# Latent attention on fp32 strips of 32 partitions, row sums by products of ones on TensorE

## Chip, cores and metric

One core of one Trainium2 chip runs the whole program. The metric is device time in microseconds, the median of a few executions. Times inside the program are counted from the start of the profiled execution's span.

## The reference

A tensor x of 2048 tokens by 128 features, fp32, goes through eight residual layers: an RWKV layer, a mixture of experts, causal attention with rotation (16 heads of 8), the mixture again, one full-attention head, a second mixture, latent attention, and that mixture again. Each is `x = x + layer(layernorm(x))`. The change concerns the seventh. Cut to what matters:

```python
q = (x @ wq).reshape(B, T, 2, 4, 128)          # 2 groups of 4 query heads
k_lat = (x @ wk_down).reshape(B, T, 2, 32)     # one latent key and value of 32 per group
v_lat = (x @ wv_down).reshape(B, T, 2, 32)
k, v = k_lat @ wk_up, v_lat @ wv_up
scores = where(causal, q @ k.T / sqrt(128), lowest)
y = softmax(scores) @ v
return y.reshape(B, T, 1024) @ wo
```

The kernel folds wk_up into wq and wv_up into wo when it starts, so that a head's query, key and value have 32 elements here.

## The kernel before

Queries are cut into NC = 4 chunks c of 512, keys into tiles kj of 128. A **unit** is one key tile against one query chunk for the four heads of a group g; causality leaves (c+1)*4 units per chunk and group, 80 in all. Of each chunk's units four lie on the diagonal and cover 512, 384, 256 and 128 queries. Scores are made with keys on partitions, exponentiated to the tile PT by ScalarE (L1418, two heads at a time), and weighted by the values on TensorE (L1374, four heads in four column strips of 32, into PSUM bank 4).

The softmax needs each query's maximum beforehand. So TensorE also makes the scores with queries on partitions, 128 queries by up to 512 keys an item (L1304, with a mask added by L1308 on the diagonal), and VectorE reduces each (L1538). These **maxima** pass through a ring of three PSUM banks (5, 6, 7): TensorE waits on `ring_free` for a bank, VectorE on `ring_full` for its data. The negated maxima are turned by TensorE and enter the scores as three more rows of the product. `make_plan` writes out one order for all engines: for each unit scores of heads 0 and 1, some ring items, scores of heads 2 and 3, some ring items, the weighting of the unit before, the rest of the ring items. Engines work in that order and wait for each other on semaphores.

The class `CausalHeads` serves this layer and the rotated one. Queries and keys are split into three bf16 parts each; the parts of four source chunks go out to a DRAM tensor (L1629) and come back stacked as 96 rows (L1598), so that one bf16 product of 96 rows holds three part products. Scores take two products a head (99 rows, the last three being the maxima, and 96 rows, L1355), a maximum takes one:

```python
for j in (2 * p, 2 * p + 1):
    for m in range(self.NP):
        r = self.rows + (3 if m == 0 else 0)
        ins = pe.matmul(k.PS[:, j, q0:CH], self.K[0:r, g % 2, j % self.kheads, m, kj * P:(kj + 1) * P],
                        self.Q[0:r, g % 2, j, m, c * CH + q0:(c + 1) * CH],
```

Row sums: GpSimd adds three heads of PT into the tile acc, VectorE the fourth (L1460, L1462), and after a chunk's last unit TensorE sums acc over partitions (L1324), VectorE takes the reciprocal of 128x512 (L1568) and multiplies (L1570), TensorE makes the output product (L1333), VectorE adds it to X (L1579). VectorE also splits the negated maxima (L1551 to L1554). Groups are the outer loop, chunks the inner. The layer norm that follows needs all four chunks.

## Time and profile before

| | us |
|---|---|
| median of 3 runs | 1944.66 |
| lowest and highest | 1942.96, 1948.3 |
| span of the profiled execution | 1933.1 |
| median less span: what lies around the span | 11.6 |
| latent stage, first projection to the next layer norm's start | 1362.5 to 1846.9 |

The profiled execution's own time is known by its span alone, from the first to the last instruction. Rows read "start, length, engine, line, operation, out<-in, shapes, count", and in brackets how long the engine had been idle and on what. PE is TensorE, DVE VectorE, ACT ScalarE, POOL GpSimd, SP the queue that issues DMAs. An fp32 product shows as two MATMUL instructions, a bf16 one as one. A row with a count is several instructions merged, from the first start to the last end.

### The profile page before, as it was taken

What the parts mean: (1) busy time and instruction counts of PE and PEld (TensorE: products, weight loads), DVE (VectorE), ACT (ScalarE), POOL (GpSimd) and SP (SyncE); (2) the same over time, 40 slices, a digit from 0 to 9 for tenths busy, and PEclk for the clock granted to TensorE, in tenths of its full rate; (3) what the DMA queues carried; (4) which work ended last, traced back from release to release, by engine and by line L of the source; (5) the groups of instructions that cost most, each with busy time, mean ns of one, the idle gap of its engine ahead of it and who ended that gap; (6) DMA issues with size and microseconds to landing.
All of it is one profiled execution on the core that took longest, in us unless ns stands there. A gap on an engine that the chain in (4) does not pass through costs nothing.

```text
span 1933.1 us, 25832 instructions
## 1 busy us (share of the span) xinstructions
PE 1601.7 (83%) x8863; PEld 807.4 (42%) x8863; DVE 1180.5 (61%) x2315; ACT 786.5 (41%) x1031; POOL 818.4 (42%) x987
## 2 busy tenths in 40 slices
PE   4766699758999899999799789989545898988779
PEld 2222466412333333332466567766212333333256
DVE  5887633578788787883333333342355878897951
ACT  2222233343565565667333344444212343334433
POOL 2224646464554635455463644000001577456900
PEclk8788699867999999999799999979656898889979
DMA  4000000151000303000000000000143000000000
GB/s 139 1 0 0 1 1 0 59 121 29 2 2 12 41 3 51 2 2 1 1 1 0 0 1 0 0 1 0 49 117 96 1 1 1 1 1 1 1 1 22
DMA packets 31585, 36.86 MB, mean 19 GB/s; under 512 B 8606, under 2 KB 24703, under 8 KB 31362
## 3 DMA queue, kind: packets, MB, share of 16 engines
q1 hardware_dynamic: 27906, 29.29, 6.4%
q10 hardware_dynamic: 3520, 6.29, 1.6%
q8 instruction: 61, 1.00, 0.2%
q14 instruction: 34, 0.28, 0.1%
q0 software_dynamic: 64, 0.00, 0.0%
HBM read 26.10 MB, written 8.91 MB: 18 GB/s over the span
## 4 chain that ended last, share of the span: by engine, by line
PE 61%; DVE 16%; DMA 7%; SPq 3%; issue 2%; ACT 2%; ACTq 0%; DVEq 0%
PE PS L943 9%; PE PS L1355 9%; PE PS L931 9%; PE PS L1304 8%; PE PS L1374 8%; DVE sb_latent_acc L1462 3%; DMA sb_rope_K<-rope_parts 3%; PE PS L1723 3%; PE PS L1741 3%; SPq L1629 2%; DVE sb_latent_mp L1538 2%; DMA latent_parts<-sb_latent_parts 2%; DVE sb_rope_mp L1538 2%; DVE sb_latent_rec L1568 1%; PE PS L1735 1%
## 5 line engine op out<-in xcount | busy, mean ns | idle before, releaser
L1538 DVE TENSOR_REDUCE sb_rope_mp<-PS 128x1 f32<-128x512 f32 (+3 forms) x560 | 345.0, 669 | 76.5 <-PE PS L1308 36.9
L1418 ACT ACTIVATE sb_rope_PT<-PS 128x1024 f32<-128x1024 f32 (+3 forms) x320 | 273.3, 895 | 223.0 <-PE PS L1359 121.7
L1462 POOL TENSOR_TENSOR sb_latent_acc<-sb_latent_acc,sb_latent_PT 128x1536 f32<-128x1536 f32 (+3 forms) x72 | 223.2, 3101 | 72.4 <-ACT sb_latent_PT L1418 68.8
L1418 ACT ACTIVATE sb_latent_PT<-PS 128x1024 f32<-128x1024 f32 (+3 forms) x160 | 140.2, 895 | 243.3 <-PE PS L1359 80.9
L995 DVE SCALAR_TENSOR_TENSOR sb_X<-PS,sb_gates,sb_X 128x128 f32 (+1 forms) x320 | 90.1, 344 | 241.3 <-PE PS L943 241.2
L1304 PE MATMUL PS<-sb_rope_K,sb_rope_Q 96*128 96x512 bf16 (+3 forms) x640 | 211.7, 371 | 30.2 <-ACT sb_rope_V L1399 18.3
L1538 DVE TENSOR_REDUCE sb_latent_mp<-PS 128x1 f32<-128x512 f32 (+3 forms) x280 | 174.3, 666 | 46.2 <-PE PS L1304 32.5
L576 POOL TENSOR_SCALAR sb_pbelow<-sb_pa,sb_ptrial 128x512 f32<-128x512 f32 x124 | 197.0, 1599 | 6.4
L583 POOL TENSOR_TENSOR sb_pbelow<-sb_pbelow 128x1024 f32<-128x1024 f32 (+1 forms) x248 | 181.7, 733 | 19.6
L931 PE MATMUL PS<-sb_HT,sb_w 128*128 (+1 forms) x384 | 182.3, 612 | 3.6 <-DVE sb_seed L514 1.9
L1355 PE MATMUL PS<-sb_rope_Q,sb_rope_K 99*128 99x512 bf16 (+3 forms) x640 | 179.4, 352 | 1.4 <-ACT sb_rope_PT L1418 0.9
L1355 PE MATMUL PS<-sb_latent_Q,sb_latent_K 99*128 99x512 bf16 (+7 forms) x640 | 160.3, 372 | 8.3 <-ACT sb_latent_PT L1418 8.3
L1304 PE MATMUL PS<-sb_latent_K,sb_latent_Q 96*128 96x512 bf16 (+3 forms) x320 | 111.4, 393 | 63.4 <-ACT sb_latent_V L1399 23.3
L1460 POOL COPY sb_latent_acc<-sb_latent_PT 128x1536 f32<-128x1536 f32 x8 | 13.2, 1655 | 335.7 <-ACT sb_latent_PT L1418 287.0
L972 ACT ACTIVATE sb_moe_hidden<-PS,sb_vec 128x512 f32<-128x512 f32 x128 | 87.8, 687 | 159.4 <-PE PS L931 155.2
L1374 PE MATMUL PS<-sb_rope_PT,sb_rope_V 128*9 128x512 f32 (+3 forms) x1280 | 148.6, 536 | 0.1
L1304 PEld LDWEIGHTS PS<-sb_rope_K,sb_rope_Q 96*128 96x128 bf16 x640 | 59.5, 99 | 181.9 <-issue 94.2
L943 PE MATMUL PS<-sb_w0b,sb_moe_hidden 128*128 128x128 f32 x1024 | 131.3, 281 | 0.0
L943 PEld LDWEIGHTS PS<-sb_w0b,sb_moe_hidden 128*128 128x128 f32 x1024 | 119.1, 191 | 14.5 <-issue 14.5
L1462 DVE TENSOR_TENSOR sb_latent_acc<-sb_latent_acc,sb_latent_PT 128x512 f32<-128x512 f32 (+3 forms) x72 | 105.3, 1463 | 10.2 <-ACT sb_latent_PT L1418 9.7
L589 POOL TENSOR_TENSOR sb_ptot<-sb_ptot,sb_prank 128x8 f32<-128x8 f32 x31 | 6.1, 198 | 226.4 <-issue 226.4
L831 POOL TENSOR_TENSOR sb_rw_kvj<-sb_rw_k,sb_rw_vj 128x512 f32<-128x512 f32 x32 | 44.3, 1389 | 133.8 <-ACT sb_rw_vj L814 96.7
(291 smaller groups left out, 2438.7 us busy)
## 6 DMA issues: line engine op xcount, KB each, us to landing
latent_parts<-sb_latent_parts SPq DMA_DIRECT2D x36, 128.0 KB
sb_rope_Q<-rope_parts SPq DMA_DIRECT2D x9, 384.0 KB
rope_parts<-sb_rope_parts SPq DMA_DIRECT2D x24, 128.0 KB, 2.4
sb_rope_tab<-in_rotation SPq DMA_DIRECT2D x1, 2048.0 KB, 8.6
sb_rope_K<-rope_parts SPq DMA_DIRECT2D x6, 256.0 KB
sb_latent_Q<-latent_parts ACTq DMA_DIRECT2D x2, 768.0 KB
sb_latent_Q<-latent_parts SPq DMA_DIRECT2D x1, 1536.0 KB, 19.1
sb_rope_Q<-rope_parts ACTq DMA_DIRECT2D x6, 192.0 KB
```

Source lines behind the costliest of these rows:

```text
L576: ch.mark(g.tensor_scalar(self.below[:, w, s, :], self.a[:, w, :], tr[:, 2 * w + s:2 * w + s + 1], None, ALU.is_lt))
L583: ch(g.tensor_tensor(bl[:, :, 0:n], bl[:, :, 0:n], bl[:, :, n:2 * n], ALU.add))
L931: pe.matmul(k.bank(b), self.w1(e, m), x, start=True, stop=True).then_inc(self.hid[b], 1)
L943: ins = pe.matmul(k.PS[:, 4 + b, i * P:(i + 1) * P], self.g[:, b, m, i * P:(i + 1) * P], self.w2(e, m), start=False, stop=(m == M - 1), sk ...
L972: s.activation(self.g[:, e % 2, m, :], k.bank(b), self.func, bias=self.b1(e, m)) \
L995: ins = v.scalar_tensor_tensor(xi, k.PS[:, 4 + b:5 + b, i * P:(i + 1) * P], gate, xi, ALU.mult, ALU.add)
L1304: ins = pe.matmul(k.PS[:, bank, at:at + w], self.Q[0:self.rows, g % 2, j, 0, q0:q0 + P], self.K[0:self.rows, g % 2, j % self.kheads, 0, kc ...
L1355: ins = pe.matmul(k.PS[:, j, q0:CH], self.K[0:r, g % 2, j % self.kheads, m, kj * P:(kj + 1) * P], self.Q[0:r, g % 2, j, m, c * CH + q0:(c ...
L1374: ins = pe.matmul(k.PS[32 * j:32 * j + self.vcols, 4, q0:CH], v, self.PT[:, u % 2, j, q0:CH], start=(kj == 0), stop=(kj == last))
L1418: s.activation(self.PT[:, u % 2, 2 * p:2 * p + 2, q0:CH], k.PS[:, 2 * p:2 * p + 2, q0:CH], ACT.Exp, scale=self.scale).then_inc(self.exps[p ...
L1462: eng.tensor_tensor(acc, acc, new, ALU.add).then_inc(self.added[who], 1)
L1538: v.tensor_reduce(self.mp[:, n % 2, kc, heads[0]:heads[-1] + 1, i], k.PS[:, bank, 0:len(heads) * w].rearrange("p (h k) -> p h k", h=len(he ...
```

## The change

`StripHeads` takes the place of `CausalHeads` for this layer. Q and K stay fp32 in SBUF and never go to DRAM: each head's 32 elements lie on partitions 32j to 32j+31, and the latent key is written four times below itself (by a weight `wkrep` that repeats its columns). A score or maximum is one fp32 product of 32 rows, a **row strip** of the array. Maxima are one head each (320 items, before 280, some of which held several heads), in head order 2, 3, 0, 1. The negated maxima, split on GpSimd, are added by a bf16 product of 3 rows a head. Masks are written first and the product added to them. Row sums are made for every unit: a ring item `part` multiplies PT by ones in four column strips, VectorE adds it to S; after a chunk two DMAs and a reciprocal of 128x16 give the factors, which `den` spreads over partitions. The order of chunks and groups is swapped (chunks outer), maxima per unit go from 4.5 to 5, PT has 3 buffers instead of 2.

```diff
+    def make_plan(self):
+...
+            if u < total:
+                plan.append((u, "scores0"))
+            plan += ring(mine[:a])
+            if u < total:
+                plan.append((u, "scores1"))
+            plan += ring(mine[a:b])
+            if 1 <= u <= total:
+                plan.append((None, ("part", u - 1)))
+                plan.append((u - 1, "weighted"))
+            plan += [(u, it) for it in relays[u]]
+            plan += ring(mine[b:])
+...
+    def pe_scores(self, pe, u, p):
+...
+        if diag:
+            for j in pair:
+                pe.matmul(k.PS[:, j, q0:q0 + P], k.identb[:, :], k.mask_kq[:, :], start=True, stop=False,
+                          skip_group_check=True)
+        for j in pair:
+            strip = slice(32 * j, 32 * j + 32)
+            pe.matmul(k.PS[:, j, q0:CH], self.K[strip, g, kj * P:(kj + 1) * P],
+                      self.Q[strip, g, c * CH + q0:(c + 1) * CH], start=not diag, stop=False, skip_group_check=True)
+        for j in pair:
+            rows = slice(32 * j, 32 * j + 3)
+            pe.matmul(k.PS[:, j, q0:CH], k.onesb[rows, :], self.negT[rows, n % 2, q0:CH], start=False, stop=True,
+                      skip_group_check=True).then_inc(self.scores[p], 1)
+...
+    def pe_item(self, pe, item, bank):
+        k, kind = self.k, item[0]
+        if kind == "max":
+            _, n, i, kc, j = item
+            c, g = self.seq[n]
+            strip = slice(32 * j, 32 * j + 32)
+            w = CH if kc < c else (i + 1) * P
+            q0 = c * CH + i * P
+            if kc == c:
+                pe.matmul(k.PS[:, bank, w - P:w], k.identb[:, :], k.mask_qk[:, :], start=True, stop=False,
+                          skip_group_check=True)
+            return pe.matmul(k.PS[:, bank, 0:w], self.Q[strip, g, q0:q0 + P], self.K[strip, g, kc * CH:kc * CH + w],
+                             start=kc < c, stop=True, skip_group_check=True)
+...
+        if kind == "part":
+...
+            for j in range(4):
+                ins = pe.matmul(k.PS[32 * j:32 * j + 32, bank, q0:CH], k.ones_col, self.PT[:, u % self.PTS, j, q0:CH],
+                                start=True, stop=True)
+            return ins
+...
+        if kind == "part":
+            n, c, g, kj, q0 = self.unit(item[1])
+            if kj == 0:
+...
+                v.tensor_copy(self.S[:, n % self.NS, :], k.bank(bank)).then_inc(free, 1)
+            else:
+                self.emptied(v, ("part", item[1] - 1))
+                v.tensor_tensor(self.S[:, n % self.NS, q0:CH], self.S[:, n % self.NS, q0:CH], k.PS[:, bank, q0:CH], ALU.add) \
+                    .then_inc(free, 1)
+...
-            a = CausalHeads(k, "latent", ln, 2, sources + [(k.wkv[:, :, :].rearrange("p a l -> p (a l)"), None)], (qb, kb), 96, 1,
-                            k.wkv[:, 1, :], 2, 32, float(P ** -0.5), k.wy, d["latent_parts"], False, True, 4.5)
+            a = StripHeads(k, "latent", ln, 5.0)
```

On TensorE, in the middle of the stage before, a full unit stands like this: a maximum (K and Q read), four products for the scores of two heads, a maximum, the other four, a maximum, and the weighting of the unit before by the values V.

```order
L1304 MATMUL PS<-sb_latent_K,sb_latent_Q 128x512
L1355 MATMUL PS<-sb_latent_Q,sb_latent_K 128x512 x4
L1304 MATMUL PS<-sb_latent_K,sb_latent_Q 128x512
L1355 MATMUL PS<-sb_latent_Q,sb_latent_K 128x512 x4
L1304 MATMUL PS<-sb_latent_K,sb_latent_Q 128x512
L1374 MATMUL PS<-sb_latent_PT,sb_latent_V 32x512 x4
```

The same place after: two maxima (L1893), the scores of two heads (L1863, strips 0 and 1) with the rows of their negated maxima (L1867), two maxima, scores of strips 2 and 3, a maximum, then the row sums by ones (L1908, cst holds them) ahead of the weighting (L1878).

```order
L1893 MATMUL PS<-sb_latent_K,sb_latent_Q 128x512 x2
L1863 MATMUL PS<-sb_latent_Q,sb_latent_K 128x512 x2
L1867 MATMUL PS<-sb_latent_negT,sb_onesb 128x512 x2
L1893 MATMUL PS<-sb_latent_K,sb_latent_Q 128x512 x2
L1863 MATMUL PS<-sb_latent_Q,sb_latent_K 128x512 x2
L1867 MATMUL PS<-sb_latent_negT,sb_onesb 128x512 x2
L1893 MATMUL PS<-sb_latent_K,sb_latent_Q 128x512
L1908 MATMUL PS<-sb_latent_PT,sb_cst 32x512 x4
L1878 MATMUL PS<-sb_latent_PT,sb_latent_V 32x512 x4
```

Eight bf16 products for scores became four fp32 and four short-rowed bf16 ones, and four column-strip products were added. At a diagonal block a mask of the full array (L1891) now stands ahead of every maximum:

```order
L1891 MATMUL PS<-sb_mask_qk,sb_identb 128x128
L1893 MATMUL PS<-sb_latent_K,sb_latent_Q 128x384
L1891 MATMUL PS<-sb_mask_qk,sb_identb 128x128
L1893 MATMUL PS<-sb_latent_K,sb_latent_Q 128x384
L1863 MATMUL PS<-sb_latent_Q,sb_latent_K 128x512 x2
```

At the start of the stage TensorE had the four chunks' projections apart, each waiting for the splitting of the one before, and the values among them; now the projections stand in a row, then the values (L1826), and the first maxima:

```order
L1819 MATMUL PS<-sb_HT,sb_wc 128x512 x2
L1822 MATMUL PS<-sb_HT,sb_wkrep 128x512 x2
L1826 MATMUL PS<-sb_wkv,sb_HT 128x64 x16
L1891 MATMUL PS<-sb_mask_qk,sb_identb 128x128
L1893 MATMUL PS<-sb_latent_K,sb_latent_Q 128x128
```

Of the plan after, counted: 39 maxima stand ahead of the first unit (32 of them diagonal ones of chunk 0), and 281 among the units, five to a unit, 96 of them diagonal. 23 of the 80 units have no maximum, the last 19 among them.

## Rows read from the trace of the kernel before

**Rows 1.** The page: span, busy time, TensorE and its granted clock in 40 slices.

```profile
span 1933.1 us, 25832 instructions
...
PE 1601.7 (83%) x8863; PEld 807.4 (42%) x8863; DVE 1180.5 (61%) x2315; ACT 786.5 (41%) x1031; POOL 818.4 (42%) x987
...
PE   4766699758999899999799789989545898988779
...
PEclk8788699867999999999799999979656898889979
```

**Rows 2.** Windows of the latent stage: busy time and instructions, granted clock, DMA share.

```profile
core 0: us, PE busy (x) PEld busy (x) DVE busy (x) ACT busy (x) POOL busy (x), PEclk, DMA share, GB/s
1362.50:1427.50 65.00, 23.35 (x56) 9.57 (x56) 15.79 (x25) 16.53 (x32) 0.00 (x0) 0.58 0.29 85
1427.50:1475.80 48.30, 26.88 (x99) 9.14 (x100) 28.99 (x59) 1.31 (x2) 0.00 (x0) 0.57 0.59 148
1475.80:1555.50 79.70, 69.56 (x419) 29.29 (x418) 69.09 (x99) 28.49 (x34) 39.75 (x16) 0.89 0.00 1
1555.50:1775.70 220.20, 191.35 (x1173) 77.14 (x1172) 182.23 (x262) 85.94 (x101) 144.50 (x49) 0.91 0.01 1
1775.70:1835.30 59.60, 46.59 (x284) 14.51 (x281) 54.13 (x22) 29.00 (x33) 50.33 (x16) 0.96 0.00 1
```

**Rows 3.** Timeline of the stage's start: start, length, instructions, idle before and releaser.

```profile
1362.51 3.78 PE L1265 MATMUL PS<-sb_HT,sb_wc 128*128 128x512 f32 x4 [0.69 <-ACT sb_HT L245]
...
1367.10 3.68 PE L1273 MATMUL PS<-sb_wkv,sb_HT 128*128 128x64 f32 x32
...
1369.31 65.97 SPq L1629 DMA_DIRECT2D latent_parts<-sb_latent_parts  x36
...
1427.58 0.29 PE L1304 MATMUL PS<-sb_latent_K,sb_latent_Q 96*128 96x128 bf16 x1 [23.29 <-ACT sb_latent_V L1399]
```

**Rows 4.** The tile of exponentials: nanoseconds least/median/most, first and last start.

```profile
L1418 ACT ACTIVATE sb_latent_PT<-PS x160: 377/1024/1042, 1475.8 to 1834.9; 128x1024 f32<-128x1024 f32 x112, 128x768 f32<-128x768 f32 x16, 128x512 f32<-128x512 f32 x16, 128x256 f32<-128x256 f32 x16
L1462 POOL TENSOR_TENSOR sb_latent_acc<-sb_latent_acc,sb_latent_PT x72: 992/3460/3819, 1482.5 to 1836.2; 128x1536 f32<-128x1536 f32 x48, 128x1152 f32<-128x1152 f32 x8, 128x768 f32<-128x768 f32 x8, 128x384 f32<-128x384 f32 x8
```

**Rows 5.** Timeline of TensorE in one full unit among maxima.

```profile
1552.93 1.06 PE L1374 MATMUL PS<-sb_latent_PT,sb_latent_V 128*32 128x512 f32 x8
...
1554.37 1.04 PE L1355 MATMUL PS<-sb_latent_Q,sb_latent_K 99*128 99x512 bf16 x4
1555.24 0.38 PE L1304 MATMUL PS<-sb_latent_K,sb_latent_Q 96*128 96x512 bf16 x1
1555.46 1.03 PE L1355 MATMUL PS<-sb_latent_Q,sb_latent_K 99*128 99x512 bf16 x4
1556.33 0.38 PE L1304 MATMUL PS<-sb_latent_K,sb_latent_Q 96*128 96x512 bf16 x1
1556.64 1.06 PE L1374 MATMUL PS<-sb_latent_PT,sb_latent_V 128*32 128x512 f32 x8
```

**Rows 6.** Timeline of a unit without maxima.

```profile
1804.78 1.94 ACT L1418 ACTIVATE sb_latent_PT<-PS 128x1024 f32<-128x1024 f32 x2 [1.91 <-DVE sb_latent_acc L1462]
...
1805.86 1.96 PE L1355 MATMUL PS<-sb_latent_Q,sb_latent_K 99*128 99x512 bf16 x8 [0.89 <-ACT sb_latent_PT L1418]
...
1808.64 1.94 ACT L1418 ACTIVATE sb_latent_PT<-PS 128x1024 f32<-128x1024 f32 x2 [1.92 <-DVE sb_latent_acc L1462]
```

**Rows 7.** VectorE, groups by line and shape: busy us, mean ns, idle before.

```profile
L1538 DVE TENSOR_REDUCE sb_latent_mp<-PS 128x1 f32<-128x512 f32 x224 | 143.7, 681 | 36.1 <-PE PS L1304 32.5 <-PE PS L1308 2.9
...
L1568 DVE RECIPROCAL sb_latent_rec<-PS 128x512 f32<-128x512 f32 x8 | 26.8, 3351 | 5.8 <-PE PS L1324 5.8
...
L1498 DVE TENSOR_TENSOR sb_latent_x<-PS,sb_latent_parts 128x512 f32<-128x512 f32 x12 | 8.3, 692 | 49.1 <-ACT sb_latent_parts L1392 49.1
```

**Rows 8.** Timeline of the stage's end.

```profile
1835.46 0.66 PE L1374 MATMUL PS<-sb_latent_PT,sb_latent_V 128*32 128x128 f32 x8 [1.48 <-ACT sb_latent_PT L1418]
...
1846.89 0.87 DVE L197 BATCH_NORM_STATS2 sb_stats<-sb_X 128x6 f32<-128x128 f32 x4 [0.31 <-DVEq L1582]
```

More of the change, by code:

```diff
@@ L98, in __init__ @@
         self.den_rope = self.cst[:, 3 * P:4 * P]
+        self.den_strip = self.cst[:, 15 * P:16 * P]
         self.ones_col = self.cst[:, 4 * P:4 * P + 32]
@@ L116, in bank @@
         return self.PS[:, b, 0:cols]
-N_CST = 5 + 8 + 2
+N_CST = 5 + 8 + 2 + 1
 class NormMemory:
@@ L290, in __init__ @@
         k.wc = sb("wc", [P, 8, 32])
+        k.wkrep = sb("wkrep", [P, 2, 4, 32])
         k.wy = sb("wy", [P, 2, P])
@@ L442, in gpsimd @@
         g.tensor_copy(k.mask_kq[:, :], k.cst[:, (6 + 8) * P:(7 + 8) * P]).then_inc(self.ready, 1)
+        for i in range(2):
+            g.tensor_copy(k.wkrep[:, i, :, :], k.wkv[:, 0, 32 * i:32 * i + 32].rearrange("p (a l) -> p a l", a=1)
+                          .broadcast_to([P, 4, 32])).then_inc(self.ready, 1)
     def tensor(self, pe):
@@ L447, in tensor @@
         pe.wait_ge(s.ready, 1)
-        pe.wait_ge(self.ready, 4)
+        pe.wait_ge(self.ready, 6)
         n = 0
@@ L1881, in constants @@
     c[:, 14 * P:15 * P] = np.where(r[:, None] > r[None, :], MASKED, 0.0)
+    c[:, 15 * P:16 * P] = (r[:, None] // 32 == r[None, :] // 32) & (r[:, None] % 32 == 0)
     c[:, CST_ORDER:] = 8 - np.arange(8)
@@ L1987, in latent_attention @@
             ln = norm()
-            qb = [(0, 0, 0, 2), (0, 64, 0, 1), (1, 0, 0, 3)]
-            kb = [(0, 0, 0, 1), (0, 32, 0, 2), (1, 0, 2, 1), (1, 32, 1, 1), (1, 64, 0, 1)]
-            sources = [(k.wc[:, 4 * g:4 * g + 4, :].rearrange("p h l -> p (h l)"), None) for g in range(2)]
-            a = CausalHeads(k, "latent", ln, 2, sources + [(k.wkv[:, :, :].rearrange("p a l -> p (a l)"), None)], (qb, kb), 96, 1,
-                            k.wkv[:, 1, :], 2, 32, float(P ** -0.5), k.wy, d["latent_parts"], False, True, 4.5)
+            a = StripHeads(k, "latent", ln, 5.0)
             with ExitStack() as arena:
@@ L2042, in scratch @@
     d["rope_parts"] = nc.dram_tensor("rope_parts", (2, 16, 3 * 8, T), BF16).ap()
-    d["latent_parts"] = nc.dram_tensor("latent_parts", (3, 4, 3 * 32, T), BF16).ap()
 def kernel(**inputs):
```

324 lines of the change are left out of this document (added).

## Prediction

> **What bounds the kernel now.** I read the page first: TensorE is busy 83% of the span and VectorE 61% [rows 1]; no other stage changes, so I looked at the latent stage in windows. It has two parts. From the first projection to the first exponential, 1362.5 to 1475.8, lie 113.3 us in which TensorE is busy 36% and 56% of the time at a granted clock of 0.57 to 0.58, and the DMA share is 0.29 and 0.59 [rows 2]. The timeline says why: the issue queue is busy with stores of the parts for 65.97 us, and the first maximum comes at 1427.58, after 23.29 us of idle [rows 3]. That is the trip through DRAM. From the first exponential, 1475.8, to the end of the last, 1835.3, lie 359.5 us for 80 units [rows 2, 4], 4.5 us a unit.
>
> In this loop the reader is to see three periods. A full unit among maxima takes 3.71 us (1552.93 to 1556.64, weighting to weighting), and TensorE stands nearly end to end in it [rows 5]: it is the bound there. A unit without maxima takes 3.86 us (1804.78 to 1808.64), while TensorE needs some 3: the chain of waits goes through the additions, and the exponential waits 1.92 us on them [rows 6]; GpSimd's take 3.46 us in the median [rows 4]. At chunk ends VectorE's reciprocals (3351 ns each) and splits stop the ring [rows 7].
>
> **Prices.** A bf16 product of 512 columns starts 0.22 us after the one before: four take 1.04, of which the last one's own record is 0.38 [rows 5]. So a record runs 0.165 beyond its streaming. Four fp32 products in column strips are eight instructions in 1.06 us [rows 5]; less 0.165 that is 0.87, two passes of 0.43 each, all four strips at once. I take 0.85 of streaming for a row strip of 32 rows too, which no row shows; alone it is four times the bf16 product of 96 rows, 0.22, that it replaces, and only four strips at once make it equal. From the end of a full-array product's streaming (1556.33 + 0.22) to the start in column strips (1556.64) lie 0.09 us [rows 5]; I take 0.09 for each change of tiling. VectorE's reduction is 0.68 in itself [rows 7], about 0.61 in a row.
>
> **Removed and gained: the start.** Two cold projections take 3.78 as now [rows 3], fourteen more at 0.86 are 12.0, the values 3.7 [rows 3], their copy 1.2: 20.7. Then 32 diagonal maxima of chunk 0: a product of 128 to 512 columns (0.21 to 0.85, mean 0.53), a mask of 0.05, two changes of tiling 0.18, and all in a row since a mask uses the whole array: 0.77 each, 25. Seven more are 4, split, turn and copy of the maxima 4, the first scores 1.3. Sum 55 to 57, against 113.3: **-57**. Nothing hides this: the first exponential waits for all of it. At the program's start 64 KB more of constants are loaded and GpSimd makes two copies more, long before their use; I put both at nothing (the whole setup waits for the constants, but they are one of many loads).
>
> **Added: the loop.** Row sums and weighting: eight column-strip products, 1.75, and two changes of tiling, 0.19: 1.94 a full unit. The rest is nine fp32 products (four scores, five maxima) and four short bf16 ones over four strips. In the order written out, the strips of maxima are 2, 3, 0, 1 round and round, five a unit, so four phases occur. If an instruction may start only when those before it have started: with the first maxima on 2 and 3 they run beside the scores of strips 0 and 1 to 0.85, the rows of maxima to 1.07; the next two need strips 0 and 1, and the second of them also the first bank of the ring, which comes free at 1.8 (data at 1.09, reduction 0.68); scores of strips 2 and 3 beside it to 2.87; the fifth to 3.7. The other three phases collide more (4.7, 4.35, 4.3), mean 4.3, a period of **6.2**. If a busy strip doesn't hold up the others, the ring still does, and I get 3.75 and **5.7**. I take 5.95. The rows show strips at once only for columns; this is the main choice.
>
> Diagonal maxima come in fours: four at 0.77, one full 0.85, two pairs of scores at 1.07, less 0.6 where a maximum's product runs beside scores, and 1.94: **7.4**.
>
> - 185 full maxima are 37 units' worth, x 5.95: 220
> - 96 diagonal ones are 19.2 units' worth, x 7.4: 142
> - masks of the 32 diagonal units, four of 0.05 and four changes each: +18
> - 14 of those units cover fewer queries, 1.6 each: -22
> - without maxima: 13 full units at 3.2 (all four scores at once 1.07, 1.94, and a wait for the second exponential), 10 short ones at 2.5: 67
> - factors, output products and turns, 3.5 for each of 8 chunks: +28. The two DMAs are five to seven units away from their use and hidden; with that cover gone they would cost about 4 a chunk.
>
> Sum 453, against 359.5: **+93.5**. VectorE has 5 x 0.61 and an addition of about 0.69 (its subtraction from PSUM has that length [rows 7]), 3.75 in a unit of 5.95: no bound any more. ScalarE has 2.0. GpSimd's additions cost nothing in the dense units that TensorE bounds, and their removal is worth 0.65 in each of 13 units; it is in the sum.
>
> **The end.** Now 11.4 us from the last weighting (1835.46) to the next statistics (1846.89), with the long reciprocal [rows 8]. After, the reciprocal is of 128x16 but two DMAs are exposed; I put it at 1 less.
>
> Together 93.5 - 57 - 1 = +35.5. Against the profiled span 1933.1 that is 1968.6; the median shown lies 11.6 above the span, so **1980 us**.
>
> **A rule weighed.** The Trainium skill (TensorEngine Tiling (Array Packing), Tiling Modes) says that changing the tiling mode drains the engine. It speaks against this change, which adds masks of the full array among row strips; the column rows agree (0.09), for row strips no row shows it. The skill (TensorE: Matmul & The Clock Gate, Part 3) gives 3.07x for four row strips, not 4x; by that the overlapped part, 37 x 3.75, would be 1.3 times as long, an estimate of 2022 in all.
>
> **Rivals.**
> - *Faster.* Changes between row strips and the full array cost nothing (128 diagonal maxima x 0.18 and 32 x 0.36: -35) and strips run at once as far as the ring lets them (5.25 a full unit: -26): 1919. The changes alone give 1945, so it decides only with both, or with either and shorter diagonal units. For it: masks are short, and weights may load behind running products. Against: the 0.09 in rows 5.
> - *No change.* A loop of 415 to 420 instead of 453 just pays back the start: 1945.
> - *Maxima don't overlap with anything*, since each waits for a bank and signals by itself: 5 x 0.85 + 2 x 1.07 + 1.94 = 8.3 a full unit, +89: 2069. For it: the rows show overlap only for products that stand in a row without waits.
> - *Row strips don't run at once at all:* 10.5 a full unit, 10.1 a diagonal one, 6.2 without maxima, together some +265: 2245. Against: column strips do.
>
> **How the numbers follow.** Chances: the forecast (slower by a few per cent) 0.45, faster 0.31, no change 0.07, maxima alone 0.11, no overlap 0.06. 0.3%, or 6 us, is about what a measurement of this kernel can tell. The range reaches from below the faster rival, 1905, to above the third, 2075. The forecast's own range is 1955 to 2020 (periods of 5.25 to 7 for a full unit). Faster 0.31, same 0.07, slower 0.62.
>
> **What would show it.** The first exponential at about 1419 instead of 1475.8, with no stores of parts. TensorE at over 0.9 in the loop, granted clock near 1. Full units with five maxima 5.7 to 6.2 apart, diagonal ones 7 or more, the last ones 3.2. A gap of about 0.09 on both sides of each mask. Two maxima of neighbouring strips starting less than 0.2 us apart. The prediction is wrong if dense full units are nearer to 5 than 6, or if masks stand in the stream without gaps.

## The result, and the profile after

| | us |
|---|---|
| before, median of 4 runs on the same chip | 1946.24 (1942.96 to 1948.3) |
| after, median of 4 runs | 2117.8 (2110.47 to 2120.16) |
| ratio, 95% interval | 1.087 (1.0836 to 1.0905) |
| span of the profiled execution after | 2108.4 |
| forecast | 1980 (1905 to 2075) |

The change costs 171 us where 35 were forecast. The direction was right, the size was not, and the range missed. In one experiment below (few row sums) three of the four executions took 32 to 50 us longer than the fourth at a lower granted clock, and the traced one is the longest of them; so no ratio is given for it, and times are compared with its fastest execution.

The page of the changed kernel, the lines that answer to [rows 1]:

```profile
span 2108.4 us, 27826 instructions
...
PE 1879.6 (89%) x10127; PEld 898.8 (43%) x10127; DVE 1092.5 (52%) x2298; ACT 782.0 (37%) x1016; POOL 587.3 (28%) x942
...
PE   5665998589998989979978998899999999999979
...
PEclk9887899769999999978999998965579788897979
```

The reader is to see two lines that part company. From the 27th slice to the 36th TensorE is busy at 9 throughout, yet its clock reads 6, 5, 5, 7, 9, 7, 8, 8, 8, 9. The windows of the latent stage show it in numbers; they answer to [rows 2]:

```profile
core 0: us, PE busy (x) PEld busy (x) DVE busy (x) ACT busy (x) POOL busy (x), PEclk, DMA share, GB/s
1368.90:1388.70 19.80, 18.47 (x66) 10.10 (x65) 5.53 (x8) 6.40 (x10) 0.95 (x1) 0.95 0.00 0
1388.70:1448.30 59.60, 59.17 (x130) 23.19 (x130) 19.53 (x41) 2.37 (x3) 1.99 (x8) 0.52 0.00 0
1448.30:1600.00 151.70, 151.70 (x688) 54.43 (x687) 56.41 (x101) 27.34 (x36) 2.00 (x8) 0.69 0.00 1
1600.00:1750.00 150.00, 150.00 (x792) 52.79 (x791) 69.91 (x122) 37.11 (x42) 2.00 (x8) 0.82 0.01 1
1750.00:1900.00 150.00, 149.29 (x864) 55.97 (x864) 72.07 (x126) 41.77 (x47) 1.00 (x4) 0.86 0.01 1
1900.00:2009.10 109.10, 108.49 (x746) 35.63 (x742) 31.53 (x51) 41.81 (x48) 1.00 (x4) 0.89 0.01 1
```

The second window is the maxima up front: TensorE busy 59.17 of 59.60 us at 0.52, which is nearly the lower of the clock's two levels (1.2 GHz). The last four are the loop of 80 units. The tile of exponentials gives its ends, as in [rows 4]:

```profile
L1955 ACT ACTIVATE sb_latent_PT<-PS x160: 383/1023/1025, 1448.3 to 2009.1; 128x1024 f32<-128x1024 f32 x112, 128x768 f32<-128x768 f32 x16, 128x512 f32<-128x512 f32 x16, 128x256 f32<-128x256 f32 x16
```

Up front, on TensorE's timeline, a mask (L1891) and one row strip (L1893) follow each other without a gap. A pair of 128 columns takes some 0.57 us at first; soon 256 columns take 1.22, where the full clock would need 0.69, as e4 below has it at that place:

```profile
1388.71 0.22 PE L1891 MATMUL PS<-sb_mask_qk,sb_identb 128*128 128x128 bf16 x1 [1.34 <-ACT sb_latent_V L1930]
1388.86 0.48 PE L1893 MATMUL PS<-sb_latent_K,sb_latent_Q 32*128 32x128 f32 x2
...
1393.58 0.29 PE L1891 MATMUL PS<-sb_mask_qk,sb_identb 128*128 128x128 bf16 x1
1393.80 1.22 PE L1893 MATMUL PS<-sb_latent_K,sb_latent_Q 32*128 32x256 f32 x2
```

In the loop the same products stand at both levels within a few microseconds of each other, again on TensorE's timeline, and again with no idle time in brackets:

```profile
1925.16 1.13 PE L1863 MATMUL PS<-sb_latent_Q,sb_latent_K 32*128 32x512 f32 x4
...
1926.35 1.06 PE L1893 MATMUL PS<-sb_latent_K,sb_latent_Q 32*128 32x512 f32 x2
1927.35 0.29 PE L1891 MATMUL PS<-sb_mask_qk,sb_identb 128*128 128x128 bf16 x1
1927.56 2.07 PE L1893 MATMUL PS<-sb_latent_K,sb_latent_Q 32*128 32x512 f32 x2
...
1929.89 2.08 PE L1863 MATMUL PS<-sb_latent_Q,sb_latent_K 32*128 32x512 f32 x4
...
1937.81 0.23 PE L1891 MATMUL PS<-sb_mask_qk,sb_identb 128*128 128x128 bf16 x1
1937.97 1.12 PE L1893 MATMUL PS<-sb_latent_K,sb_latent_Q 32*128 32x512 f32 x2
1939.02 0.23 PE L1891 MATMUL PS<-sb_mask_qk,sb_identb 128*128 128x128 bf16 x1
```

Two strips of scores take 1.13 at 1925.16 and 2.08 at 1929.89; one maximum 1.06 and then 2.07. At 1937.81 the full clock is back: mask and maximum take 1.21 there. Where no diagonal block is near, a full unit among maxima stands like this, the place that answers to [rows 5]:

```profile
1851.18 1.07 PE L1908 MATMUL PS<-sb_latent_PT,sb_cst 128*32 128x512 f32 x8
1852.06 1.04 PE L1878 MATMUL PS<-sb_latent_PT,sb_latent_V 128*32 128x512 f32 x8
1853.03 0.70 PE L1893 MATMUL PS<-sb_latent_K,sb_latent_Q 32*128 32x512 f32 x2
1853.05 0.69 PE L1863 MATMUL PS<-sb_latent_Q,sb_latent_K 32*128 32x512 f32 x1
...
1856.59 1.07 PE L1908 MATMUL PS<-sb_latent_PT,sb_cst 128*32 128x512 f32 x8
```

The period is 5.41 (1851.18 to 1856.59), and a maximum and a score product on different strips start 0.02 apart. That is the shortest one. Which strips the five maxima meet changes from unit to unit, and other full units without masks at the full clock take 5.9: 1783.98 to 1789.88, 1872.52 to 1878.41, and this one:

```profile
1916.13 1.06 PE L1908 MATMUL PS<-sb_latent_PT,sb_cst 128*32 128x512 f32 x8
...
1922.03 1.07 PE L1908 MATMUL PS<-sb_latent_PT,sb_cst 128*32 128x512 f32 x8
```

Units without maxima are 3.44 and 3.15 apart in turn, read off the exponentials (1986.56, 1990.00, 1993.15; [rows 6] has 3.86), and the end of the stage takes 10.06 from the last weighting to the statistics, against 11.43 in [rows 8]:

```profile
1986.56 1.94 ACT L1955 ACTIVATE sb_latent_PT<-PS 128x1024 f32<-128x1024 f32 x2 [1.21 <-PE PS L1867]
1990.00 1.94 ACT L1955 ACTIVATE sb_latent_PT<-PS 128x1024 f32<-128x1024 f32 x2 [1.50 <-PE PS L1867]
```

```profile
2010.12 0.40 PE L1878 MATMUL PS<-sb_latent_PT,sb_latent_V 128*32 128x128 f32 x8
...
2020.18 0.87 DVE L198 BATCH_NORM_STATS2 sb_stats<-sb_X 128x6 f32<-128x128 f32 x4 [0.32 <-DVEq L2051]
```

**Where the time went.** The loop takes 560.8 us between the first and the last exponential (before 359.1). Since TensorE is busy all the time, length times granted clock says how long it would be at the full clock: 151.7 x 0.69 + 150 x 0.82 + 150 x 0.86 + 109.1 x 0.89 = 453.8, to some 3 us, since the clock is given to two digits. The forecast sum for the loop was 453. So 107 us are the clock's. Up front it is 59.6 x (1 - 0.52) = 28.6 more. 35.5 forecast and 135.6 for the clock are 171.1; the stage grew by 166.9 (484.4 to 651.3), and 8.4 of the two spans' difference of 175.3 lie outside it, 6.4 of them ahead of it (it starts at 1368.9 instead of 1362.5), in layers that the change doesn't touch; why was not traced.

The theory to test, **clock**: TensorE's granted clock falls where single row strips of 32 rows run one at a time, even with masks of the full array between them and though the engine never idles. Its rivals: **work** (masks, changes of tiling or overlap cost more than forecast, and the clock is a bystander), and **gaps** (waits too short to show in the busy line let the clock fall).

### The profile page after: what moved, and what is told of

Read it like the earlier page. It is cut to its first block, busy times and chain, and to the rows that moved or that the text cites. A ratio compares the mean times of both kernels' runs of the same rounds, so it can differ in the third digit from the quotient of the medians.

```text
span 2108.4 us, 27826 instructions
## 1 busy us (share of the span) xinstructions
PE 1879.6 (89%) x10127; PEld 898.8 (43%) x10127; DVE 1092.5 (52%) x2298; ACT 782.0 (37%) x1016; POOL 587.3 (28%) x942
## 4 chain that ended last, share of the span: by engine, by line
PE 78%; DVE 8%; DMA 2%; ACT 2%; issue 1%; SPq 0%; ACTq 0%; DVEq 0%
PE PS L1893 12%; PE PS L948 9%; PE PS L936 8%; PE PS L1379 6%; PE PS L1309 6%; PE PS L1863 6%; PE PS L1360 5%; PE PS L1908 4%; PE PS L1878 4%; PE PS L2134 3%; PE PS L2152 3%; DVE sb_H L223 1%; DMA sb_rope_K<-rope_parts 1%; DVE sb_rope_mp L1543 1%; PE PS L2146 1%
## 5 line engine op out<-in xcount | busy, mean ns | idle before, releaser
L2013 DVE TENSOR_REDUCE sb_latent_mp<-PS 128x1 f32<-128x512 f32 (+3 forms) x320 | 187.9, 608 | 268.0 <-PE PS L1893 267.5
L1893 PE MATMUL PS<-sb_latent_K,sb_latent_Q 32*128 32x512 f32 (+3 forms) x640 | 301.3, 694 | 0.1
L1309 PE MATMUL PS<-sb_rope_K,sb_rope_Q 96*128 96x512 bf16 (+3 forms) x640 | 211.3, 369 | 28.6 <-ACT sb_rope_V L1404 18.1
L1863 PE MATMUL PS<-sb_latent_Q,sb_latent_K 32*128 32x512 f32 (+3 forms) x640 | 189.9, 642 | 0.6 <-ACT sb_latent_PT L1955 0.6
L1309 PEld LDWEIGHTS PS<-sb_rope_K,sb_rope_Q 96*128 96x128 bf16 x640 | 59.6, 99 | 179.3 <-issue 91.0
L1893 PEld LDWEIGHTS PS<-sb_latent_K,sb_latent_Q 32*128 32x128 f32 x640 | 100.5, 222 | 63.0 <-issue 40.6
L936 PEld LDWEIGHTS PS<-sb_HT,sb_w 128*128 128x128 f32 x384 | 71.0, 199 | 71.3 <-issue 68.0
L1908 PE MATMUL PS<-sb_latent_PT,sb_cst 128*32 128x512 f32 (+3 forms) x640 | 95.6, 677 | 0.7 <-DVE sb_latent_mp L2013 0.7
L2031 DVE TENSOR_TENSOR sb_latent_S<-sb_latent_S,PS 128x512 f32<-128x512 f32 (+3 forms) x72 | 43.1, 598 | 93.2 <-PE PS L1908 92.8
```

The source lines that it names most:

```text
L936: pe.matmul(k.bank(b), self.w1(e, m), x, start=True, stop=True).then_inc(self.hid[b], 1)
L1309: ins = pe.matmul(k.PS[:, bank, at:at + w], self.Q[0:self.rows, g % 2, j, 0, q0:q0 + P], self.K[0:self.rows, g % 2, j % self.kheads, 0, kc ...
L1863: pe.matmul(k.PS[:, j, q0:CH], self.K[strip, g, kj * P:(kj + 1) * P], self.Q[strip, g, c * CH + q0:(c + 1) * CH], start=not diag, stop=Fal ...
L1893: return pe.matmul(k.PS[:, bank, 0:w], self.Q[strip, g, q0:q0 + P], self.K[strip, g, kc * CH:kc * CH + w], start=kc < c, stop=True, skip_g ...
L2013: v.tensor_reduce(self.mp[:, n % 2, i, j:j + 1, kc], k.PS[:, bank, 0:w], AX.X, ALU.max).then_inc(free, 1)
```

## The experiments

In the table, the loop is the stretch from the first to the last exponential, and its length at full clock the sum over the same kind of windows as above. In c1 TensorE waits part of the time, so that the sum says nothing there; for e10 it was not taken.

| kernel | median us | ratio to before (95%) | loop | at full clock |
|---|---|---|---|---|
| changed | 2117.8 | 1.087 (1.0836 to 1.0905) | 560.8 | 454 |
| e1, no masks of maxima | 1947.72 | 1.0017 (0.9996 to 1.0037) | 426.3 | 406 |
| e2, masks together | 2047.38 | 1.0517 (1.048 to 1.0553) | 515.8 | 434 |
| e3, few row sums | 2135.9 (fastest 2102.39) | not given | 611.9 | 391 |
| e4, eight masks | 2085.21 | 1.0763 (1.0698 to 1.0828) | 535.1 | 495 |
| e5, no masks, few row sums | 1912.37 | 0.983 (0.9759 to 0.9901) | 402.3 | 354 |
| e6, no masks, GpSimd sums | 1943.32 | 0.9995 (0.996 to 1.003) | 416.5 | 376 |
| e7, no masks, pairs | 1925.05 | 0.9917 (0.9889 to 0.9944) | 367.9 | 363 |
| e8, masks, pairs | 2085.64 | 1.0747 (1.0715 to 1.0779) | 488.2 | 419 |
| e9, no masks, pairs, GpSimd | 1897.15 | 0.9744 (0.9699 to 0.979) | 343.0 | 337 |
| e10, e9 and wide products up front | 1930.91 | 0.9925 (0.9889 to 0.9961) | 346.2 | |
| c1, before without masks of maxima | 1923.83 | 0.9908 (0.9873 to 0.9944) | 356.1 | |

**m1, patterns alone.** A small program in which TensorE does nothing but rows of products, 90 full bf16 products (L27) ahead of each pattern. It was executed once. The comments are added here.

```diff
+    for i in range(times):              # row_f32, strips 1, 2 or 4
+        j = i % strips
+        r = slice(32 * j, 32 * j + 32)
+        ins = pe.matmul(PS[:, 2 + j, 0:cols], xf[r, 0:P], xf[r, P:P + cols], start=True, stop=True)
+    for i in range(times):              # masked_f32, a mask and one strip in turns
+        pe.matmul(PS[:, 2 + j, cols - P:cols], xb[:, 0:P], xb[:, P:2 * P], start=True, stop=False, ...)
+        ins = pe.matmul(PS[:, 2 + j, 0:cols], xf[r, 0:P], xf[r, P:P + cols], start=False, stop=True, ...)
```

> This kernel computes nothing of the reference: x is copied to the output, and TensorE runs nine patterns of products for some 20 to 30 us each at the full clock, 90 full-array bf16 products of 512 columns (about 19.5 us) ahead of each. Theory A (the clock): in the changed kernel the granted clock fell to its lower level while TensorE had work all the time, so a pattern of single fp32 row strips back to back should itself show the clock near 0.5, with 0.85 us a product becoming 1.7, and the same for single strips with a full-array mask between; four row strips at once and full-array fp32 should stay near 1. Theory B (gaps): the clock falls only where TensorE waits for other engines, so every pattern here, which waits for nothing, stays near 1.

Windows, one for each pattern: one strip, two strips, four strips, the full array in fp32, four column strips, a mask and one strip in turns:

```profile
30.90:88.70 57.80, 57.80 (x73) 22.06 (x73) 0.00 (x0) 0.00 (x0) 0.53 0.00 0
110.40:136.20 25.80, 25.80 (x120) 11.32 (x120) 0.00 (x0) 0.00 (x0) 1.00 0.00 1
155.80:177.40 21.60, 21.60 (x201) 10.13 (x200) 0.00 (x0) 0.00 (x0) 1.00 0.00 1
197.00:222.60 25.60, 25.60 (x61) 11.20 (x60) 0.00 (x0) 0.00 (x0) 1.00 0.00 0
242.20:268.00 25.80, 25.80 (x241) 7.66 (x240) 0.00 (x0) 0.00 (x0) 1.00 0.01 1
287.50:349.00 61.50, 61.50 (x109) 20.67 (x107) 0.00 (x0) 0.00 (x0) 0.53 0.00 0
```

TensorE is busy all of every window. One strip alone runs at 0.53 (57.87 us for 36 products, 1.61 each); two strips in turn at 1.00, 0.43 each; four at 1.00, 0.217 each, four at once; mask and strip (384 columns) in turns at 0.53, 1.79 a pair after 1.00 for each of the first three (287.49, 288.48, 289.48). The timeline has one more pair, the same column form that the row sums use, but on one strip, and one bf16 row strip:

```profile
370.35 45.66 PE L34 MATMUL PS<-sb_xb 32*128 32x512 bf16 x120
...
476.83 31.09 PE L52 MATMUL PS<-sb_x 128*32 128x512 f32 x72
```

120 bf16 products on one row strip take 0.38 each, where 0.22 is the full clock's pace; 36 fp32 products on one column strip 0.86 each, the full clock's. So neither fp32 nor strips as such bring the clock down, but one row strip at a time does. Gaps aren't needed for it: there are none here.

**e1, no masks of the maxima.** The one edit; the maximum over a whole diagonal block only shifts the softmax.

```diff
-            if kc == c:
-                pe.matmul(k.PS[:, bank, w - P:w], k.identb[:, :], k.mask_qk[:, :], start=True, stop=False, ...)
...
-                             start=kc < c, stop=True, skip_group_check=True)
+                             start=True, stop=True, skip_group_check=True)
```

> The changed kernel without the masks ahead of the maxima: each maximum is then taken over the whole diagonal block, later keys too, which shifts the softmax but leaves its value. 128 masks and 256 changes of tiling go. At the full clock that is 128 x (0.05 + 0.18) = 30 us, and some 15 more because maxima of neighbouring strips can run at once. Theory A: the clock also stays up where it fell, so most of the 135 us that the clock cost comes back: 1960 to 2010 us. Theory B (the tiling changes and their waits alone cost): 2118 - 45 = about 2070, with the granted clock in the loop still near 0.8.

Measured 170 us less than the changed kernel, below even the clock theory's 1960 to 2010. Windows from the first exponential on:

```profile
1418.60:1600.00 181.40, 180.38 (x1184) 73.48 (x1183) 100.91 (x184) 53.82 (x66) 3.03 (x12) 0.89 0.01 1
1600.00:1750.00 150.00, 149.29 (x1056) 59.80 (x1056) 91.80 (x159) 50.57 (x57) 2.02 (x8) 1.00 0.01 1
1750.00:1844.90 94.90, 94.06 (x754) 33.24 (x750) 33.09 (x56) 43.37 (x50) 1.01 (x4) 1.00 0.01 1
```

At full clock the loop lost 47 us (454 to 406), what masks and changes of tiling cost as work; its length fell by 134.5. The other 87 are the clock, back at 1.00 from 1600 on. Up front 29 more went (79.4 to 50.5 from first projection to first exponential), half of it work; there the clock did not come back: it is 0.52 from 1388 to 1430, without a single mask of a maximum.

**c1, a control:** the kernel before with the same masks left out, in this layer and in the rotated one.

```diff
-                                start=True, stop=kc < c)
-                if kc == c:
-                    ins = pe.matmul(k.PS[:, bank, at + w - P:at + w], k.identb[:, :], k.mask_qk[:, :], ...)
+                                start=True, stop=True)
```

> The kernel before with the masks of its diagonal maxima left out (the maximum over the whole diagonal block shifts a softmax by more, the result is the same). Its products have 96 rows. Theory clock: masks there sit between products of 96 rows, which do not let the clock fall, so only their work goes, 128 x 0.053 or less than 7 us, mostly beside VectorE: 1938 to 1944, within 0.3% of before. Rival (a mask costs as much anywhere, 170 us / 128 = 1.3 us each as in the changed kernel): 1944 less tens of us, under 1900.

1% faster overall, more than the clock theory expected, and far from the rival. In the latent loop, the only place that compares with e1, it is 3.0 us (359.1 to 356.1), at a granted clock of 0.91 in both. A mask between products of 96 rows costs little. The two traced executions differ by 6.1 us in all, 3.0 in this loop and 2.9 ahead of the stage; the rest of the 20 us between the medians is in no trace.

**e2, masks together:** the masks of up to three neighbouring diagonal maxima first, then their strips.

```diff
+                for x, it in enumerate(group):
+                    pe.matmul(k.PS[:, 5 + self.bank_of(ring + x)[0], w - P:w], k.identb[:, :], k.mask_qk[:, :], ...)
+                for x, it in enumerate(group):
+                    self.pe_item(pe, it, 5 + b).then_inc(self.ring_full[b], 1)
```

> The changed kernel with up to three diagonal maxima in a row issued together: wait for their ring banks, write their masks, then their fp32 products on up to three strips at once. All masks remain, but the changes of tiling go from two for each maximum to two for two or three, and the strips run side by side. Theory A: the clock rises where strips run at once; 1990 to 2050. Theory B: 128 x 0.12 = 15 us saved in changes, about the same again from overlap, less longer waits for the ring: 2080 to 2110.

70 us less than the changed kernel with the same products. The traces differ by 57: 20 of work and 25 of clock in the loop, 10 up front, where the first exponential came at 1438.2 instead of 1448.3. The rest is in no trace (of the changed kernel the fastest execution was traced, of e2 the slowest). Letting strips stand together is worth much, but masks still part the groups.

**e3, few row sums:** the sums of only the first unit of each chunk are made, so the factors are incomplete.

```diff
-                plan.append((None, ("part", u - 1)))
+                if self.units[u - 1][1] == 0:
+                    plan.append((None, ("part", u - 1)))
```

> The changed kernel with the product of ones and VectorE's addition made for the first unit of each chunk alone: 8 instead of 80. The row sums leave out all other key tiles, so the output is wrong by a factor a query. 72 groups of column strips go, at the full clock 0.43 to 0.87 each, together 56 us. If TensorE bounds the loop, the time falls by 56 us or somewhat more at a mixed clock: 2050 to 2062. Theory A adds: column strips of 128 rows are what keeps the clock up between single row strips, so without them it may fall further and the gain be under 30.

Two of its windows:

```profile
1600.00:1750.00 150.00, 150.00 (x540) 53.21 (x540) 48.55 (x85) 31.66 (x35) 1.00 (x4) 0.58 0.00 1
1750.00:1900.00 150.00, 150.00 (x621) 53.73 (x613) 51.77 (x89) 33.68 (x40) 2.00 (x8) 0.62 0.00 1
```

63 us of work at full clock are gone, yet even the fastest execution, 2102.39, is only 15 us below the changed kernel's median and 8 below its fastest, with a granted clock of 0.843 over the whole program against 0.866 to 0.872. In the traced one, the longest, the loop is 51 us longer than the changed kernel's, and the clock is 0.58 and 0.62 where it was 0.82 and 0.86. The column-strip products of the row sums had been holding it up. Work alone asks for 2050 to 2062, which no execution came near.

**e4, more work on purpose:** every mask is written eight times.

```diff
-                pe.matmul(k.PS[:, bank, w - P:w], k.identb[:, :], k.mask_qk[:, :], start=True, stop=False, ...)
+                for _ in range(8):
+                    pe.matmul(k.PS[:, bank, w - P:w], k.identb[:, :], k.mask_qk[:, :], start=True, stop=False, ...)
```

> Every mask ahead of a diagonal maximum is written eight times instead of once: 128 x 7 = 896 more bf16 products of the full array and 128 columns, 0.053 us each at the full clock, 47.5 us of work that gives nothing. Theory clock (TensorE's clock falls where one row strip of 32 rows runs at a time, with nothing wider beside it, though the engine never idles): the wide products between them hold the clock up; up to 135 us of the loss come back for 48 paid, so the time falls below the changed kernel's 2118, to some 2035 to 2080, with a granted clock above 0.92 in the loop. Rival work (each mask costs its work and a change of tiling, and the clock is an effect of something else): 2118 + 48 to 56, some 2165 to 2175. Rival half: the clock rises a little, the two cancel, 2110 to 2130.

The window of the maxima up front and one of the loop, and TensorE's timeline up front:

```profile
1390.30:1443.50 53.20, 52.45 (x376) 29.85 (x373) 19.46 (x41) 2.37 (x3) 1.99 (x8) 0.91 0.00 1
...
1600.00:1750.00 150.00, 150.00 (x1059) 63.38 (x1056) 72.97 (x127) 38.79 (x45) 2.00 (x8) 0.95 0.01 1
```

896 products that give nothing made the kernel 33 us faster (by the ratios, 1.087 and 1.0763, each against the kernel before on its own chip, some 21): 41 us more of work in the loop at full clock, and a loop 26 us shorter. The maxima up front run at 0.91 instead of 0.52:

```profile
1394.49 0.69 PE L1894 MATMUL PS<-sb_latent_K,sb_latent_Q 32*128 32x256 f32 x2
1395.12 0.62 PE L1892 MATMUL PS<-sb_mask_qk,sb_identb 128*128 128x128 bf16 x8
```

256 columns take 0.69 (1.22 in the changed kernel), and the pair with its eight masks 1.18, less than the 1.36 with one mask there (1393.58 to 1394.94). Work and changes of tiling can't give that, since both grew. The median came out 5 us above the expected 2035 to 2080.

**e5 and e6, less work without masks.** e5 is e1 and e3 together; its sums are incomplete. e6 gives two units of three in chunks 1 to 3 to GpSimd, complete:

```diff
+        self.by_pool = [kj % 3 != 0 and self.seq[n][0] > 0 for n, kj in self.units]
...
+            if self.seq[n][0]:
+                rests[end + 2].append(("pool", n))
...
+            eng.tensor_tensor(acc, acc, new, ALU.add).then_inc(self.pooled, 1)
```

> Leaves out the masks of the diagonal maxima and, of the row sums, all units but the first of each chunk (the sums are then incomplete): 72 ring items of four fp32 products in column strips go, about 64 full ones x 0.97 (with the change of tiling) = 62 us at the full clock. Theory work (without masks TensorE runs at the full clock and bounds the loop): 1947 - 62, less what the chain through the exponentials takes over in the 23 units without maxima (some 10): 1885 to 1900. Theory clock (those column-strip products use the whole array and carry the clock of the row strips; without them the clock falls as it fell in the kernel with few row sums and masks, which got no faster): granted clock in the loop below 0.95 and a time of 1915 to 1960.

> A candidate to beat both: no masks of the diagonal maxima, and two units of three in chunks 1 to 3 (46 of 80) are summed by GpSimd, idle here, into one tile of four heads x 512, which TensorE sums once a chunk (6 items more). 40 items of row sums less on TensorE, 0.97 each, less some short ones: -36 at the full clock, so 1947 - 36 = 1911 if the clock stays near 1 (theory work). GpSimd needs 4.6 us for an addition of 2048 elements (four thirds of 3.46), 9.2 for three units; those take 12 or more among maxima and 9.6 without, so it should just keep up. Theory clock: with fewer column-strip products the clock falls and eats the gain, 1925 to 1960.

Of e5's 53 us less work in the loop 24 arrived, of e6's 30 only 10. e5's 1912 lies between the two theories, nearer to the clock's 1915; e6's 1943 is inside the clock's range and 32 above that of work. Both times the clock gave way in the middle, 1600 to 1750: 0.84 and 0.85, against 1.00 in e1. e6's window:

```profile
1600.00:1750.00 150.00, 149.28 (x872) 56.41 (x870) 76.97 (x133) 47.41 (x54) 60.79 (x26) 0.85 0.01 1
```

**e7, e8, e9, the order.** Four maxima a unit instead of five, so that 76 stand up front instead of 39, two behind the scores of heads 0 and 1 and two behind those of heads 2 and 3, so that four neighbours lie on four strips. e7 is without masks, e8 with them, e9 is e7 with e6's sums. All three have four buffers of negT instead of two.

```diff
-            a, b = (len(mine) + 3) // 4, (len(mine) + 1) // 2
+            a, b = min(2, len(mine)), min(4, len(mine))
...
-            a = StripHeads(k, "latent", ln, 5.0)
+            a = StripHeads(k, "latent", ln, 4.0)
```

> No masks of the diagonal maxima, and the order written so that four neighbouring products always lie in four different row strips: four maxima a unit (rate 4 instead of 5), two of them behind the scores of heads 0 and 1 (on strips 2 and 3) and two behind those of heads 2 and 3 (on strips 0 and 1). 76 maxima stand up front instead of 39 (37 x some 0.65, which VectorE's reductions set, +24), 61 units carry four, 19 none. Theory overlap (row strips run at once when neighbours differ): a unit takes 2 x (0.85 + 0.22) + 1.94 = 4.1, or 4.4 where VectorE's four reductions and one addition and the three banks press; loop 61 x 4.1 to 4.4 + 19 x 3.2 + 28 = 340 to 357 against 426 in the kernel without masks, granted clock near 1: 1947 + 24 - 86 to - 69 = 1885 to 1902. Rival (the strips already run at once as far as the ring lets them, so order tells nothing, only the count of products does): 1935 to 1955.

> The same order and rate with the masks of the diagonal maxima in place. Theory clock: beside a mask of the full array each diagonal strip still runs alone, so the clock falls there as in the changed kernel, up front above all (76 instead of 39 maxima, all but the first units' at half the clock); between diagonal blocks the order helps. 1.08 to 1.09 of the kernel without masks: 2020 to 2070. Rival (the order is what cost, the masks their work of some 0.23 each = 30): 1915 to 1935.

> No masks, the paired order, and two units of three in chunks 1 to 3 summed by GpSimd, as in the run with GpSimd before. TensorE's need falls to 2 x 1.07 + 1.94/3 + 1.06 x 2/3 = 3.5 in the mean of a unit with maxima; GpSimd needs 3.1 in the mean, VectorE 4 x 0.61 + 0.23 = 2.7. Theory overlap with the clock kept: 40 x 0.9 = 36 less than the paired kernel, some 1850 to 1870. Theory clock against it: with less wide work the clock falls below 0.95 in the middle, as it did with GpSimd in the old order (0.85 there), and the gain is eaten: 1880 to 1900. Rival GpSimd (its additions now hold up PT's buffers): exponentials wait on them, 1890 to 1920.

Windows of e7 up front and in the loop, then of e9 in the loop:

```profile
1392.00:1453.90 61.90, 60.24 (x167) 33.33 (x166) 38.49 (x75) 2.97 (x4) 2.99 (x12) 0.51 0.00 1
1453.90:1700.00 246.10, 245.12 (x1949) 96.27 (x1952) 154.35 (x277) 90.04 (x111) 4.01 (x16) 0.98 0.01 2
```

```profile
1452.50:1600.00 147.50, 146.84 (x1128) 57.48 (x1131) 91.25 (x164) 57.60 (x71) 50.13 (x27) 0.96 0.01 2
1600.00:1700.00 100.00, 98.05 (x750) 37.43 (x746) 60.40 (x108) 39.98 (x47) 52.00 (x19) 1.00 0.01 2
```

e7's loop is 58 us shorter than e1's, less than the expected 69 to 86, and the start of the stage takes 30 us more (80.7 against 50.5) instead of 24, since the 76 maxima up front run at 0.51: 1925 where 1885 to 1902 was expected. Part of the loop's gain is only moved: 37 maxima went from the loop to the front, and start and loop together are 28 us shorter (476.8 to 448.6). How much of that is the order and how much the rate of four was not tried apart. Yet it is 23 us below e1, which the rival (1935 to 1955) did not allow. e9 now keeps the gain that e6 lost: with strips in pairs the clock stays at 0.96 to 1.00 with 46 units' row sums on GpSimd, and the loop is 25 us shorter than e7's. 1897.15 is 2.6% below the kernel before, the best here; it missed its 1850 to 1870 mostly because e7, from which that was counted, did. The time alone would fit both rivals (1880 to 1900 and 1890 to 1920); the clock in the loop speaks against the first, and 25 of 26 us of work arriving against the second. e8 puts the masks back into e7: 161 us more, 16 above its 2020 to 2070, 105.2 us up front at 0.51, and 0.80 and 0.90 in the loop. The order alone doesn't hold the clock.

**Where the theory falls short.** Up front neither e1 nor e7 nor e9 has a mask, the maxima go over the four strips in turn, and TensorE is busy nearly throughout (60.24 of 61.90 us in e7), yet the clock is 0.50 to 0.52, where m1's two or four strips in turn ran at 1.00. So "different strips" is not enough there. What differs from m1 is the ring of three banks and VectorE behind it. An estimate: VectorE takes 0.68 for 512 columns [rows 7], a strip of 128 to 512 columns 0.22 to 0.86 (m1's 0.86 scaled by columns), so at the full clock little more than one strip would be at work at a time. No run tested that.

**e10, wide work where it should help e9:** ahead of every fourth maximum up front eight products of the full array.

```diff
+                if ring < 76 and ring % 4 == 0:
+                    for i in range(8):
+                        pe.matmul(k.PS[:, 3, i % 4 * P:(i % 4 + 1) * P], k.identb[:, :], k.mask_qk[:, :], start=True, stop=True)
```

> The fastest kernel so far (paired order, no masks, GpSimd sums; 1897) with work added that gives nothing: ahead of every fourth of the 76 maxima up front, eight bf16 products of the full array and 128 columns into a score bank that is idle then, 19 x 8 = 152 products, 0.42 us for eight at the full clock plus two changes of tiling, 0.6. Up front takes 61.5 us at a granted clock of 0.50 there, 1.02 us a maximum. Theory clock: the wide products bring the clock back to over 0.9 up front; VectorE's reductions (0.69) then set the pace, 4 x 0.69 + 0.6 = 3.4 for four instead of 4.1, so some 50 to 54 us, total 1885 to 1890, faster though it does more. Rival (too little wide work, the clock stays at half): 19 x 1.05 = 20 us more at half clock, less what the ring hides, total 1908 to 1917.

```profile
1391.00:1465.00 74.00, 62.74 (x262) 27.48 (x261) 30.30 (x64) 1.02 (x1) 2.01 (x8) 0.53 0.00 1
```

The rival won, and by more than it asked for (1930.91, asked 1908 to 1917): the clock stayed at 0.53, TensorE now also waits (62.74 busy of 74.00), and the stage's start took 113.3 us (1373.5 to 1486.8) against 83.3 in e9. The same eight products that lifted the clock in e4 ahead of every strip did not do so ahead of every fourth. The run changed the pattern too: with three banks in the ring, three strips now start together and the fourth waits for VectorE (0.50 idle at 1397.08, 0.77 at 1406.88) and runs alone before the next wide products, so waits and lone strips may have a part in it. A filler isn't a cure in itself.

## Why the prediction was wrong

The step that failed is the one written as "TensorE at over 0.9 in the loop, granted clock near 1". Every term of the sum, 220 for full maxima, 142 for diagonal ones and the rest, was priced at the full clock. TensorE was busy (559.48 of 560.8 us), but the granted clock was 0.81. As work the sum is 453 against 453.8, closer than its terms are, so partly luck; as time the loop came out 107 longer, and the maxima up front 28.6. No rival named the clock. [rows 2] show 0.57 to 0.58 where TensorE waits and 0.89 to 0.96 in the loop, where it is busy 78 to 87% of the time; no row of before had a single row strip of 32 rows, and the forecast gave no reason why such a stream should keep the clock. m1 shows that the clock also falls with a TensorE that never waits, and e3 and e4 that this is what costs the time here.

- **The start.** First projection to first maximum 19.8, forecast 20.7. The maxima up front, 59.6 at 0.52, are 31 at full clock; forecast 25 + 4 and what hangs on them (4 + 1.3), some 34. The start gained 33.9 (113.3 to 79.4) instead of 57.
- **A change of tiling.** The forecast was 0.09 each way. From a mask's start to the strip's lie 0.16 (1937.81 to 1937.97), less its own 0.05 some 0.11; from there to the next mask 1.05 (to 1939.02), less the strip's 0.86 some 0.19. Both ways are 0.30 instead of 0.18: a mask and a maximum of 512 columns take 1.21 at full clock and were put at 1.08. m1 says the same: 1.00 for mask and 384 columns is 0.05 + 0.65 + 0.30. The rival without that cost was wrong, and the term was too low, an estimate of 12 us over the loop's 96 diagonal maxima.
- **Overlap of strips.** Shown for different strips (0.02 apart) and in m1 (0.217 each for four). Full units take 5.41 in one case and 5.9 in the three others named above, against the forecast's 5.95 (5.7 to 6.2), which had foreseen that they differ by phase. So the main choice was right, though the one unit of 5.41 meets the prediction's own sign of being wrong (nearer to 5 than 6).
- **Without maxima** 3.44 and 3.15 in turn, forecast 3.2. **The end** gained 1.4, forecast 1. Both right.
- **Small slips.** 1.06 less 0.165 is 0.895 and not 0.87; m1's four column strips take 0.865 (25.96 us for 30 groups of four), so the price taken was right. And the 11.6 us added to the span are not what lies around it: every execution whose span is on record took 1.8 to 2.3 more than its span. The rest is that the traced execution of before was some 9 us faster than the median. It did little harm, since that of the changed kernel was 7 faster too (2110.47 against 2117.8).
- **Maxima don't overlap** and **no overlap**: both refuted by the same rows, though 2118 lies between the times that they gave. A time alone would have spoken for the wrong mechanism.

The Trainium skill (TensorEngine Tiling (Array Packing), Tiling Modes) has the drain at a change of mode; the 0.11 and 0.19 on the rows are in keeping with it. The Trainium skill's figure of 3.07x for four row strips (TensorE: Matmul & The Clock Gate, Part 3) is not what m1 shows in a long stream of fp32 products: 0.864 for a full-array product and 0.217 on four strips are 3.97x.

## What to carry to other kernels

Multiply busy time by granted clock before believing it, and ask how each new kind of product runs alone: a stream of single products of 32 rows runs at half the clock however full it is. Short pieces that keep strips from standing side by side (here a mask of 0.05 us that the result doesn't need) can cost far more than their work, and taking wide work out of such a stream may bring little or nothing. So write the order first, with neighbours on different strips, and take work off TensorE afterwards: then it paid in full in the loop (25 of 26 us, e9), before it did not (10 of 30, e6). Look at the maxima up front as well: there the order alone did not bring the clock back.

## What the runs showed of the hardware that was not expected

- With no idle time at all, one fp32 or bf16 row strip of 32 rows, or a mask and such a strip in turns, brought TensorE to its lower level, 1.2 GHz (0.53 in the mean of 58 and 61 us). Two strips in turn, four, the full array, four column strips, and one column strip stayed at 2.4 GHz.
- Adding 896 products to such a stream made the whole kernel 33 us faster (e4). Taking 72 items of four products away, 63 us of work, brought 15 us in the fastest execution, and in the traced one, the longest of four, the loop was 51 us longer (e3).
- Strips in turn don't always keep the clock: with three PSUM banks and VectorE behind them, the unmasked maxima up front ran at 0.50 to 0.52 (e1, e7, e9).
- The Trainium skill (TensorE: Matmul & The Clock Gate, HAM oscillation — how this bites in real kernels) tells of the gate as a matter of gaps between products. m1 has the fall without any.
- What it is in a row strip that the clock follows was not measured; the runs order patterns, they don't explain them.
